# Second feed-forward of a three-block layer: from a block of its own into the last steps of the attention's stream

## The reference, cut to what matters

```python
def reference(...):                                  # x: (1, 1024, 512)
    x = x + _L0_attn_a_ref(_layernorm(x), ...)       # rotary attention, 32 heads of 16
    x = x + _L0_ffn_ref(_layernorm(x), ...)          # feed-forward 1
    x = x + _L0_attn_b_ref(_layernorm(x), ...)       # 32 heads of 128, 8 key heads, causal, linear bias
    x = x + _L0_ffn_ref(_layernorm(x), ...)          # feed-forward 2, same weights as 1

def _L0_ffn_ref(x, W_base, b_base, W_router, lora_A, lora_B):      # 512 -> 512, 8 experts of rank 16, top 2
    probs = softmax(xf @ W_router.T)
    topk_p, topk_i = top_k(probs, 2); topk_p /= sum(topk_p)
    w = sum(one_hot(topk_i, 8) * topk_p[..., None], axis=1)
    h = einsum('td,erd->ter', xf, lora_A)
    lora_out = einsum('ter,eor,te->to', h, lora_B, w) * 2.0
    return x @ W_base.T + b_base + lora_out
```

## Time and profile before

| | us |
|---|---|
| median of 3 runs | 1658.74 (1657.24 to 1659.19) |
| the profiled execution | 1659.02 |
| its span in the profile | 1657.1 |
| PE busy | 1520.1 (92% of the span) |
| DVE busy | 1119.1 (68%) |
| ACT busy | 814.6 (49%) |
| POOL busy | 393.0 (24%) |
| mean granted TensorE clock | 0.973 of full speed |

### The profile page before, as it was taken

The page is one execution under the profiler, slowest core; times in us unless marked ns, Lnnn a source line. Parts: engine busy times, 40 slices in busy tenths (PEclk is TensorE's granted clock), DMA queues, the critical chain, the costliest instruction groups (busy, mean ns, idle before and its releaser), DMA issues. The chain is left out here.

```text
span 1657.1 us, 25384 instructions
## 1 busy us (share of the span) xinstructions
PE 1520.1 (92%) x8968; PEld 1179.2 (71%) x8968; DVE 1119.1 (68%) x2853; ACT 814.6 (49%) x2108; POOL 393.0 (24%) x360
## 2 busy tenths in 40 slices
PE   3947999999898799999999999999999999999969
PEld 2834444443587688888888888888888888888757
DVE  5635777774376577677677677677767767767745
ACT  3510555556433455555555555556455555555521
POOL 4101100001253231322323133133133133131130
PEclk9977999999999899999999999999999999999979
DMA  3341533321100100100100010010010010000011
GB/s 145 98 127 28 68 40 40 44 36 53 42 29 1 39 27 1 39 14 13 34 6 26 1 39 26 1 39 27 1 39 27 1 39 18 10 1 1 1 45 51
DMA packets 43231, 54.53 MB, mean 33 GB/s; under 512 B 6368, under 2 KB 25056, under 8 KB 43104
## 3 DMA queue, kind: packets, MB, share of 16 engines
q1 hardware_dynamic: 42144, 52.52, 12.9%
q10 hardware_dynamic: 960, 0.39, 0.1%
HBM read 44.31 MB, written 8.39 MB: 32 GB/s over the span
## 5 line engine op out<-in xcount | busy, mean ns | idle before, releaser
L1690 ACT ACTIVATE prob<-prob,ab_neg_max 128x128 f32<-128x128 f32 (+7 forms) x256 | 201.1, 786 | 254.0 <-DVE ab_neg_max L1797 253.0
L1814 DVE TENSOR_TENSOR ab_pt_l<-ps,ab_pt_h 128x512 fp32r<-128x512 f32 x288 | 198.1, 688 | 73.7 <-ACT ab_pt_h L1718 72.9
L1718 ACT CAST ab_pt_h<-ps 128x512 fp32r<-128x512 f32 x288 | 171.6, 598 | 109.2 <-PE ps L1603 108.6
L1797 DVE CUSTOM_DVE_ANT_0 prob<-ps,rel 128x512 f32<-128x512 f32 (+3 forms) x256 | 146.1, 571 | 100.8 <-PE ps L52 100.0
L1019 DVE TENSOR_REDUCE ra_part_max<-ps 128x1 f32<-128x128 f32 (+1 forms) x336 | 164.9, 551 | 50.0 <-PE ps L919 32.3
L50 PE MATMUL ps<-ab_w_h,ab_xt_h 128*128 128x512 f32 (+1 forms) x512 | 186.3, 364 | 6.6 <-DVE ab_v_l L1834 6.0
L1603 PE MATMUL ps<-ident,prob 128*128 128x128 f32 x1152 | 173.5, 273 | 5.8 <-DVE ab_qt_l L1806 4.5
L1822 DVE TENSOR_SCALAR prob<-prob,ab_recip 128x128 f32<-128x128 f32 (+7 forms) x256 | 168.5, 658 | 9.1
L52 PE MATMUL ps<-ab_w_h,ab_xt_l 128*128 128x512 f32 (+1 forms) x512 | 174.1, 340 | 0.0
L51 PE MATMUL ps<-ab_w_l,ab_xt_h 128*128 128x512 f32 (+1 forms) x512 | 173.5, 339 | 0.0
L1603 PEld LDWEIGHTS ps<-ident,prob 128*128 128x128 f32 x1152 | 138.0, 140 | 26.7 <-DVE ab_qt_l L1806 5.8
(11 more groups left out here) (252 smaller groups left out, 3462.8 us busy)
## 6 DMA issues: line engine op xcount, KB each, us to landing
f_raw<-in_wqkv SPq DMA_DIRECT2D x32, 384.0 KB, 3.8
f_raw<-in_wbo SPq DMA_DIRECT2D x32, 256.0 KB, 2.6
parts<-pa_stage SPq DMA_DIRECT2D x12, 256.0 KB, 3.0
parts<-f_raw SPq DMA_DIRECT2D x12, 256.0 KB, 3.4
ra_q_st<-parts SPq DMA_DIRECT2D x24, 128.0 KB, 6.1
ra_k_st<-parts SPq DMA_DIRECT2D x24, 128.0 KB, 6.5
ra_first_rows<-parts SPq DMA_DIRECT2D x24, 128.0 KB, 7.1
ra_first_rows<-parts SPq DMA_DIRECT2D x84, 32.0 KB, 1.9
```

Of the source, the lines that this page charges most:

```text
L1690: act.activation(prob[:, t % 2, h, 0:w], prob[:, t % 2, h, 0:w], ACT.Exp, bias=neg_max[:, t % 2, h, pieces_per_head(t % NT) - 1:pieces_per ...
L1718: act.copy(pt_h[:, n % PT, :], ring_bank("p", u, j)).then_inc(pt_high, 1)
L1797: dve.tensor_tensor_reduce(out=prob[:, t % 2, h, k0:k1], in0=ps[:, n % 2, a:b], in1=const["rel"][:, SLIDE - i * P + k0:SLIDE - i * P + k1] ...
L1814: dve.tensor_tensor(pt_l[:, n % PT, :], ring_bank("p", u, j), pt_h[:, n % PT, :].bitcast(F32), ALU.subtract).then_inc(emptied, 1)
```

## The change

`ffn_block` is gone. Feed-forward 2 becomes tiles 8 to 15 of the same `TileFeedForward` and `TileNorm` objects that did feed-forward 1. Its calls are attached to the end of each slot, as `second(half, q)`: a half is four slots, q the slot in it. From step 61 (`SECOND`) on, each half takes in one tile, by the table `SECOND_TILES`; a tile's moments and centring are in its first half, turn and hidden part in the next (a), main part, weighted turn and finish in the one after (b), the add in the one after that (c). What is left after step 65 (halves 9 to 12) is issued behind the stream. The weights are loaded by SP behind those of the last key head, split in steps 60 and 61, and lie in the columns of `xt` that are no longer read and in rows of `v`. The ring of banks shrinks from three to two from step 61 on, since bank 6 is needed to turn the tiles; banks 2 and 3 (of the projections) take the hidden and main parts.

```diff
+SECOND = B_STEPS - 3
+SECOND_TILES = (0, 1, 2, 3, 4, 5, None, 6, None, 7)
+SECOND_HALVES = len(SECOND_TILES) + 3
+def second_tiles(half, *lags):
+    at = [SECOND_TILES[half - lag] if 0 <= half - lag < len(SECOND_TILES) else None for lag in lags]
+    return [i if i is None else NT + i for i in at]
...
-            bank = min(banks[:max(1, t)], key=lambda b: last.get(b, -1))
+            bank = min(banks[:max(1, t) if t <= last_full else 2], key=lambda b: last.get(b, -1))
...
-    job_of = shared_jobs(SHARED, MIXED)
+    job_of = shared_jobs(SHARED, MIXED, SECOND - 1)
...
+        s_rooms = [(xt_h[:, k, 0:F_N], xt_l[:, k, 0:F_N]) for k in range(KC)]
+        sb_room = tuple(v[:, 4:4 + C // DB, :].rearrange("p r n -> p (r n)") for v in (v_h, v_l))
...
+        def half_of(t, s):
+            return 2 * (t - SECOND) - 1 + s // 4, s % 4
...
# SP, behind the loads of the last key head
+            for k in range(KC):
+                load(S_PIECES + k, ins["wf"][k * P:(k + 1) * P, :])
+            load(S_PIECES + KC, ins["wb"])
+            for i in range(NT):
+                sp.wait_ge(ff.added, NT + i + 1)
+                sp.dma_start(out_dram[i * P:(i + 1) * P, :], x[:, i, :]).then_inc(out_stored, 16)
...
# POOL
+            def second(half, q):
+                v, b = second_tiles(half, 0, 2)
+                if q == 1 and b is not None:
+                    ff.route(pool, b)
+                if q == 2 and b is not None:
+                    ff.offset(pool, b)
+                if q == 3 and v is not None:
+                    f_norm.invert(pool, v)
...
# PE
+            def second(half, q):
+                a, b = second_tiles(half, 1, 2)
+                if q == 0 and a is not None:
+                    if a == NT:
+                        pe.wait_ge(emptied, last_in_third + 1)
+                        pe.wait_ge(scaled, B_STEPS)
+                    f_norm.turn(pe, a, (ff.ht_low, second_before(half - 2)))
+                if q == 1 and b is not None:
+                    ff.main(pe, b)
+                if q == 2 and a is not None:
+                    ff.hidden(pe, a)
+                if q == 3 and b is not None:
+                    ff.turn_weighted(pe, b, (f_norm.low_done, second_before(half)))
+                    ff.finish(pe, b)
...
# ACT
+            def second(half, q):
+                a, b = second_tiles(half, 1, 2)
+                if q == 0 and b is not None:
+                    ff.weigh(act, b)
+                if q == 1 and a is not None:
+                    if a >= NT + 2:
+                        act.wait_ge(ff.summed, a - 1)
+                    f_norm.high(act, a)
+                if q == 3 and b is not None:
+                    ff.high_weighted(act, b)
+                if q == 3 and a is not None:
+                    ff.take_hidden(act, a)
...
+                    if t == SECOND - 1 and s < KC:
+                        act.wait_ge(projected, KC * (SECOND + 1))
+                        split_high_of(S_PIECES + s)
...
# DVE
+            def second(half, q):
+                v, a, b, c = second_tiles(half, 0, 1, 2, 3)
+                if q == 0 and c is not None:
+                    ff.add(dve, c)
+                if q == 0 and b is not None:
+                    ff.rank(dve, b)
+                if q == 1 and b is not None:
+                    ff.divide(dve, b)
+                if q == 1 and a is not None:
+                    f_norm.low(dve, a)
+                if q == 2 and v is not None:
+                    dve.wait_ge(emptied, job_of["o", B_STEPS - 2 * NT + v][0] + 1)
+                    f_norm.moments(dve, v)
+                if q == 3 and b is not None:
+                    ff.low_weighted(dve, b)
+                if q == 3 and v is not None:
+                    f_norm.centre(dve, v)
...
# every engine, behind the last step
+            for half in range(2 * (B_STEPS + 2 - SECOND) - 1, SECOND_HALVES):
+                for q in range(4):
+                    second(half, q)
...
-        with ExitStack() as own:
-            ffn(own, "f2")(out_dram)
```

More of the change, by code:

```diff
@@ L239, in turn @@
         for k in range(KC):
-            last = pe.transpose(self.bank[:, k * P:(k + 1) * P], self.xn[:, k * P:(k + 1) * P], self.const["ident"][:, :])
+            last = pe.transpose(self.bank[:, k * P:(k + 1) * P], self.xn(i)[:, k * P:(k + 1) * P], self.const["ident"][:, :])
         last.then_inc(self.turned, 1)
@@ L259, with __init__ @@
     NH = 256
-    def __init__(self, nc, ctx, own, tag, x, norm, weights, w, wb, banks, const):
+    def __init__(self, nc, ctx, own, tag, x, norm, weights_in, w, wb, banks, const):
         def sb(name, shape, dt=F32):
@@ L1311, in shared_jobs, with second_before, stream_block @@
     return place
-def stream_block(nc, ctx, x, prob, o_all, wo, f_room, f_raw, f_raw_in, const, ps, ins):
+SECOND = B_STEPS - 3
[4 more added lines that the diff above has]
+    return [i if i is None else NT + i for i in at]
+def second_before(half):
+    return NT + sum(i is not None for i in SECOND_TILES[:max(0, half)])
+def stream_block(nc, ctx, x, prob, o_all, wo, f_room, f_raw, f_raw_in, const, ps, ins, out_dram):
     def sem(name):
@@ L1642, in step @@
                         project_out(t - 2)
+                    second(*half_of(t, s))
             def middle(m):
@@ L1676, in _, with split_high_of @@
                     step(m - LEAD)
+            for half in range(2 * (B_STEPS + 2 - SECOND) - 1, SECOND_HALVES):
+                for q in range(4):
+                    second(half, q)
         @block.scalar
         def _(act):
-            def split_high_of(n, of_output):
-                k = n % KC
-                high = wo_h if of_output else w_h
-                src = raw[:, k, 0:C] if of_output else raw[:, k, :]
-                act.wait_ge(raw_in[k], 16 * (n // KC + 1))
-                act.copy(high[:, k, :], src).then_inc(split_high, 1)
+            def split_high_of(n):
+                columns, high, _ = raw_of(n)
+                act.wait_ge(raw_in[n % KC], 16 * (n // KC + 1))
+                act.copy(high, raw[:, n % KC, 0:columns]).then_inc(split_high, 1)
+            def second(half, q):
[10 more added lines that the diff above has]
+                    ff.take_hidden(act, a)
             def exponent(t, h):
```

289 lines of the change are left out of this document (67 added, 222 removed).

## The result

The changed kernel takes 1661.86 us (median of 13 runs, 1660.76 to 1665.3) against 1657.74 for the one before beside it (1655.05 to 1660.81): ratio 1.0028, 95% interval 1.002 to 1.0037. It is slower by 0.28%, 5.6 us above the forecast.

A forecast was written before the change was run, and what follows sets the result against it. PE (92% busy) bounds the kernel, with some 17 us almost without PE work behind the stream. Steps 61 to 65 add 41.8 us; a tail of 18.7 gives span 1652.2, clock 2.5 more, 1654.7; forecast 1656.3 us, range 1647 to 1664.

The forecast's parts named there:

- PE work that moves: Steps 62 to 65: feed-forward tiles at 5.5 us each add 7.35, 11.0, 11.0 and 5.5 us of PE work.
- what hides it: Steps 62 to 64: PE's existing idle room absorbs 0.3, 1.8 and 0.6 us of the added work.
- Loads and splits: SP's weight loads and the splits on ACT and POOL in steps 60 and 61: cost 0, at most 1 us.
- The smaller ring: Two banks make slot 2's first turned block wait for the queries: 1.7 us in step 61, 1.1 in step 62.
- The new waits: Steps 62 to 65: PE waits before finishes, for adds, the bank ring and centring; 3.1 us in step 65.
- step 62's term of +9.2: Lengthening of step 62: 7.35 of PE work plus waits of 1.1 and 1.1, less 0.3 of room filled.
- The tail: Behind the stream's last matmul one chain through DVE, POOL, PE and ACT to the final store: 18.7 us at full clock.
- The clock: Step 65 and the tail: one and a half slow-clock spells cost 2.5 us, with ends of 0 and 11.4.
- The clock falls and stays down: Rival, chance 0.13: half clock from tile 6's turn in step 65 through the tail costs 11.4 us, giving 1665.3.
- POOL blocks DVE: Rival, chance 0.15: normalisings or centrings meeting POOL operations lose 0.6 us each, eight halves, +4.8 us, giving 1661.
- The waits are covered: Rival, chance 0.22: half of roughly 15 us of waits is taken back and the clock stays up, giving 1647.
- What would show it: Signs: last projection near 1634, idle about 1 us before finishes, tail 19 to 22 us; against: stream end before 1628 or after 1640.

The follow-up runs named there:

- repeated run: The changed kernel run again as it is, as the measure for the other runs: 1662.42 us, ratio 1.0030 to the kernel before.
- third bank kept: Changed kernel with the job ring keeping three banks for one step more, through step 61: 1661.77 us, ratio 1.0024 to the kernel before.
- High copy first: Changed kernel with ACT's high copy of the turned tile in quarter 0 of each half instead of quarter 1: 1660.92 us, ratio 1.0024.
- the waits filled: Changed kernel with 112 idle matmuls added in PE's waits in steps 62 to 65 and the tail: 1657.88 us, ratio 0.9998.
- the order of DVE and POOL mended: Changed kernel with weighted turn and copies in quarter 2, next tile's moments before DVE's low weighted copy, POOL's offset in quarter 0: 1652.49 us.
- the mended order: Changed kernel with third bank through step 61, early weighted turn, high copy first, moments before DVE's low weighted copy, offset in quarter 0: 1649.16 us.

## Why the prediction was wrong

The forecast was a gain of 2.4 us; measured was a loss of 4.1. Three terms of the sum failed: the waits, the clock, and the weight splits, which stood in it at 0. Counted from the end of step 60, as in the table, the forecast was 1652.2 - 1520.24 = 132.0 us at full clock and 134.5 with the slow clock. Measured: 135.1 at full clock, and 140.3 to 141.3. So steps 61 to 65 and the tail were forecast 3.1 us too short at full clock, the price of the clock 2.7 to 3.7 too small, and step 60 adds 1.3: 7.1 to 8.1 us together, where the medians say 6.5 (-2.4 against +4.1) and the ratio of the repeated run 7.4.

- *PE work that moves* and *what hides it*: nearly held. Step 64, which has two whole tiles and no slow clock, was forecast 25.0 and takes 24.84, so the test that the text named (23 to 27) was met; in part by luck. Its waits are 0.87 + 0.16 + 1.49 = 2.5 for the 3.55 forecast, and without waits it takes 22.3 for 21.5. The starts of PE's instructions give 11.3 for the work of two tiles instead of 11.0, and 0.2 of room filled instead of 0.6. Step 63 at full clock (third bank kept) is alike: waits of 3.98 for 3.95, 26.7 without them for 26.0.
- *Loads and splits*, "cost 0": failed. Step 60 takes 16.92 instead of 15.62 us. That a copy of a turned block might come late was named, with at most 1 us; it does, behind ACT's split and behind a normalising that took 1.50 instead of 0.55 beside POOL's. No run undoes the splits, so the two parts are read from the trace alone.
- *The smaller ring*, step 61: forecast +1.7; the wait is 1.66 and goes with the third bank (18.59 to 16.74).
- *The new waits*: step 62's term of +9.2 failed. With the 1.9 us of finish put into the next stretch, steps 62 to 65 were forecast 23.1, 29.9, 25.0 and 17.0; at full clock they take 25.24, 30.65, 24.87 and 17.58. In slot 2 of step 62 I took 1.16 + 1.1 = 2.26; it is 3.15. The step that failed is "now one score and one block earlier: 1.1": I moved only PE's instructions, and didn't ask what the change puts ahead of the queries' copies in the queues of ACT and DVE. High copy first took 1.05 off this wait. The wait for centring ahead of the second turn (0.42 to 0.7) was not in the sum either; the remaining 0.5 or so is PE work a little longer and no room filled, as in steps 63 and 64. In slot 3 of step 63 the wait is 3.11 for 2.6.
- *The tail*: forecast 18.7 at full clock, 18.15 measured with the waits filled, by the chain that the text gave.
- *The clock*: this term failed most. "One and a half such spells, 2.5" was worked out for step 65 and the tail alone. There are four, in steps 62, 63, 65 and the tail, and they cost 5.2 to 6.2. I held that idles of 1.16 and 1.01 us had left the clock up, and did not price the waits of 2.3 and 2.6 us that stood in my own sum against it. The page "TensorE: Matmul & The Clock Gate", section "A second HAM failure mode: psum-queue depth-cycling", of the Trainium skill, which the text set aside, tells of another kernel in which short idles between groups of matmuls make the clock go down and up. With the filled waits as the test, this case agrees for idles of 1.5 to 3.2 us; those of about 1 us in the kernel before left the clock full.
- *The rivals.* *The clock falls and stays down*, the one that ends slower, named the right mechanism, but neither its place nor its extent: steps 62 and 63 had slow stretches too, the clock came back between the stretches, and its price stayed below the 8 us named as deciding. It was the three errors together that turned a gain of 2.4 us into a loss of 4.1. *POOL blocks DVE* was minor for the offset (0 to 1.2 us); it also has a share, which no run here separates, in the 1.3 us of step 60. The page "SBUF — State Buffer" of the Trainium skill, section "Who interferes with whom", agrees with the centring that took 1.47 us and the normalising that took 1.50: both began behind the POOL operation and ended just behind it. The centring of 1.67 us fits it less well, since by the profile it began 0.10 us ahead of POOL's offset. *The waits are covered* didn't happen: nothing in the order lay beneath the finishes. Where one puts the hidden part there, 9.9 us go with the order of DVE and POOL mended.
- *What would show it*: the finish waits (0.87, more in slot 3 of step 63), slot 2 of step 61 and a tail of 19 to 22 us were as named. The stream's end at 1640.92 is past the 1640 that was to speak against the forecast.

What isn't settled: how the 1.3 us of step 60 divide between ACT's queue and POOL beside DVE; why a wait of 3.11 us in step 63 leaves the clock up with the third bank kept and not without it, and why the 2.10 of step 62 was followed by 3.6 us at half rate in the mended order and by none in the high-copy run. No run here separates it.

## What to carry to other kernels

When a stage is folded into a stream that keeps PE full, count what it puts into every engine's list of work ahead of the stream's own copies, the splits of its weights included, and not only PE's work; and put an instruction that PE can do between each result that makes a round through ACT and DVE and the matmul that reads it. Look at the granted clock behind every new wait of PE, and judge an edit by the whole section, since a slow stretch removed in one step came back in another. Start that section before the first instruction that the change adds: here step 60 was left out, and with it 1.3 us. Filling the waits with matmuls that change nothing is a cheap test of what the clock costs; mending the order was worth more.

## What the runs showed that I had not expected

- Granted clock and idle time: the clock was still full in waits of 3.1 and 3.0 us and 0.56 and 0.52 in the 3.4 and 3.2 us of work behind them. The slow time of a step was 3.1 to 3.6 or 6.7 to 7.0 us in all steps of the stream that had any.
- Removing an unrelated wait of 1.66 us in step 61 took 3.2 us of slow time out of step 63 and put 3.8 and 3.5 into steps 62 and 65.
- A centring of 0.54 us took 0.81 to 1.67 beside POOL's operations; the one of 1.47 us ended just behind the offset that it met (1623.57 against 1623.29).
